# Conv-preact spectral block on one core: images 0 to 3 of the next batch loaded during the attention, and the "+1" of the scaling factors moved from GpSimd to ScalarE

## The reference

```
n    = groupnorm(x)                     # 32 groups of 8 columns, over all images and rows
xn   = instance_norm(n)                 # per image
k, q = spectral_conv(xn) -> 64 x 64     # low modes only, 8 x 8 corners
v    = spectral_conv(xn) -> 256 x 256
att  = softmax(q k^T * 64) v            # over the 64 images of a batch
att  = instance_norm(att) + n
mix  = spectral_conv(instance_norm(att), 32 x 32 corners)
skip = instance_norm(att) * w
out  = instance_norm(instance_norm(mix + skip)) + att
y    = x + out
```

## Time and profile before

| | us |
|---|---|
| median of 3 runs (range) | 658.64 (658.28 to 662.75) |
| profiled execution: its own time | 657.47 |
| its span in the trace | 655.5 |
| busy: PE / DVE / ACT / POOL | 619.2 / 486.5 / 336.7 / 356.0 |
| transfers | 136.32 MB |
| PE's granted clock, mean of the execution | 0.988 of full speed |

### The profile page before, as it was taken

The page is one execution under the profiler, slowest core; times in us unless marked ns, Lnnn a source line. Parts: engine busy times, 40 slices in busy tenths (PEclk is TensorE's granted clock), DMA queues, the critical chain, the costliest instruction groups (busy, mean ns, idle before and its releaser), DMA issues.

```text
span 655.5 us, 14804 instructions
## 1 busy us (share of the span) xinstructions
PE 619.2 (94%) x5584; PEld 556.6 (85%) x5584; DVE 486.5 (74%) x1095; ACT 336.7 (51%) x730; POOL 356.0 (54%) x430
## 2 busy tenths in 40 slices
PE   9999899899999899989999999989999989996994
PEld 8999798699999889879999878978898987985773
DVE  4666876788776777678777767768887778768896
ACT  6888343465665523365666634256576662333331
POOL 0260035969970013897993002498899000369995
PEclk9999999999999999999999999999999999997998
DMA  9991000999999400399999910069999970004686
GB/s 322 335 386 56 1 1 7 313 314 331 302 308 326 161 1 1 102 341 302 315 338 304 319 39 1 2 240 309 334 292 320 314 249 1 1 33 174 252 311 259
DMA packets 72215, 136.32 MB, mean 208 GB/s; under 512 B 5905, under 2 KB 6417, under 8 KB 72145
## 3 DMA queue, kind: packets, MB, share of 16 engines
q1 hardware_dynamic: 72144, 135.38, 60.9%
HBM read 68.25 MB, written 67.11 MB: 206 GB/s over the span
## 4 chain that ended last, share of the span: by engine, by line
PE 55%; DVE 15%; DMA 10%; POOL 10%; ACT 3%; issue 3%; SPq 3%; POOLq 0%; DVEq 0%; ACTq 0%
PE psY L354 21%; PE psP L408 12%; POOL X L801 8%; PE psY L377 7%; DMA X<-in_x 6%; PE psT L393 5%; DMA out<-X 4%; DVE QP L889 4%; DVE Y L853 3%; ACT SQ L566 3%; PE psP L377 2%; SPq L324 2%; DVE SQ L853 1%; PE psP L454 1%; DVE X L853 1%
## 5 line engine op out<-in xcount | busy, mean ns | idle before, releaser
L801 POOL TENSOR_TENSOR X<-X,ALPHA 128x512 f32<-128x512 f32 x244 | 254.4, 1078 | 17.4 <-DVE IM L1086 15.4
L354 PE MATMUL psY<-FWD,X 128*128 128x128 f32 x2048 | 247.8, 279 | 10.3 <-DMA X<-in_x 10.2
L354 PEld LDWEIGHTS psY<-FWD,X 128*128 128x128 f32 x2048 | 234.9, 192 | 26.4 <-issue 18.5
L889 DVE TENSOR_REDUCE QP<-SQ 128x32 f32<-128x512 f32 x256 | 162.2, 679 | 49.6 <-ACT SQ L566 49.4
L853 DVE TENSOR_TENSOR X<-X,psP 128x512 f32<-128x512 f32 x192 | 126.3, 684 | 54.3 <-PE psP L408 24.7
L566 ACT ACTIVATE SQ<-X 128x512 f32<-128x512 f32 x256 | 146.2, 621 | 14.7 <-DMA X<-in_x 7.4
L408 PE MATMUL psP<-INVW,T 64*128 64x256 f32 x768 | 141.1, 402 | 9.5 <-DVE X L853 8.6
L779 POOL TENSOR_TENSOR Y<-Y,OMEGA 128x256 f32<-128x256 f32 x32 | 23.8, 743 | 192.1 <-ACT Y L570 191.9
L588 ACT ACTIVATE T<-psT,BIA,SCL 128x256 f32<-128x256 f32 x128 | 65.3, 560 | 108.9 <-PE psT L393 104.3
L408 PEld LDWEIGHTS psP<-INVW,T 64*128 64x128 f32 x768 | 93.1, 190 | 28.7 <-issue 12.4
L558 ACT ACTIVATE Y<-psY 128x512 f32<-128x512 f32 x128 | 76.2, 596 | 57.1 <-PE psY L354 56.6
(11 more groups left out here) (197 smaller groups left out, 446.4 us busy)
## 6 DMA issues: line engine op xcount, KB each, us to landing
X<-in_x SPq DMA_DIRECT2D x116, 512.0 KB, 5.4
out<-X SPq DMA_DIRECT2D x116, 512.0 KB, 4.8
X<-in_x SPq DMA_DIRECT2D x24, 256.0 KB, 3.9
out<-X SPq DMA_DIRECT2D x24, 256.0 KB, 3.5
INVH<-t_inv_h SPq DMA_DIRECT2D x1, 256.0 KB, 9.0
LW<-in_low_w SPq DMA_DIRECT2D x1, 204.0 KB, 7.5
GWT<-t_w SPq DMA_DIRECT2D x1, 192.0 KB, 9.8
FWD<-t_fwd SPq DMA_DIRECT2D x1, 128.0 KB, 2.2
```

What stands on the lines that cost most here:

```text
L354: last = mm(psY[p % 2][:, (2 * i + c) * 128:(2 * i + c + 1) * 128], X[:, 2 * p + i, a, c * 128:(c + 1) * 128], FWD[:, a, :], start=a == 0, ...
L801: P.tensor_tensor(v, v, al, MUL).then_inc(x_scaled, 1)
L889: V.tensor_reduce(QP[:, 4 * (k % 2) + place(n) % 4, :], SQ[:, n % RING, :].rearrange("p (a g j) -> p g a j", a=HC, j=GW), AX.XY, ADD).then ...
```

## The change

`AHEAD = 4` images of the next batch are loaded a second time. While the attention of batch b runs, SP waits until GpSimd has added groups 0 to 4 of `S`, and loads images 0 to 3 of batch b+1 with one transfer of 1 MB into `Y[:, 1, 0, 8:40, :]`, the place of the weighted modes of groups 1 to 4. The forward transform and the squares of these four images read that copy. Their ordinary load into `X`, after the store of the old images, stays where it was; GpSimd's scaling waits for it now.

For the factors, GpSimd now does only the product `c * r`; a new ScalarE instruction adds the one (`add_one`, semaphore `one_added`). GpSimd makes the product of group g+1 inside group g, ahead of its third image (ahead of the seventh in group 4), and that of group 0 ahead of the last `add_products` of the attention. ScalarE's `add_one` of group g+1 stands in unit 2g, behind `keep_t` (in unit 9 for group 5), in every batch.

```diff
+        AHEADf = Y[:, 1, 0, 8:8 + 8 * AHEAD, :].rearrange("p i u -> p (i u)").rearrange("p (i n) -> p i n", n=HC * W)
+        AHEADx = AHEADf.rearrange("p i (a w) -> p i a w", a=HC)
...
+        def image(nb, n):
+            return AHEADx[:, n, :, :] if nb and n < AHEAD else X[:, n, :, :]
+
+        def flat_image(nb, n):
+            return AHEADf[:, n, :] if nb and n < AHEAD else Xf[:, n, :]
+
+        def image_in(nb, n):
+            return (ahead_in, 16 * nb) if nb and n < AHEAD else (loaded(n), 16 * nb + 16)
...
             def batch(b, more):
+                if more:
+                    sp.wait_ge(products, 8 * b + 1 + AHEAD)
+                    sp.dma_start(AHEADf, x_v[b + 1, :, 0:AHEAD, :]).then_inc(ahead_in, 16)
                 for q in range(PAIRS):
...
-                    pe.wait_ge(loaded(2 * p + i), 16 * nb + 16)
+                    pe.wait_ge(*image_in(nb, 2 * p + i))
...
-                act.wait_ge(loaded(n), 16 * nb + 16)
+                act.wait_ge(*image_in(nb, n))
...
-                nc.scalar.activation(SQ[:, n % RING, :], Xf[:, n, :], ACT.Square).then_inc(squared, 1)
+                nc.scalar.activation(SQ[:, n % RING, :], flat_image(nb, n), ACT.Square).then_inc(squared, 1)
...
+            def add_one(b, g):
+                act.wait_ge(alpha_made, 8 * b + g + 1)
+                al = ALPHA[:, g % 2, :, :].rearrange("p i g -> p (i g)")
+                nc.scalar.activation(al, al, ACT.Identity, bias=ONES[:, 0:1], scale=1.0).then_inc(one_added, 1)
...
                 mode_powers(b, SPLIT)
+                add_one(b, 0)
                 low_piece(b, 0)
...
+                    if u < 2 * NG - 2 and u % 2 == (u // 2 == SPLIT - 1):
+                        add_one(b, u // 2 + 1)
                     if not more and u in (2, second(b) + 5):
                         vector_alphas(b, int(u > 2))
...
             def alphas(b, g):
 
-                al = ALPHA[:, g % 2, :, :]
-                P.tensor_tensor(al, over(MR[:, 5, 0:1], [[0, 8], [1, GROUPS]]),
+                if g in (0, SPLIT):
+                    pool.wait_ge(c2_kept, 2 * b + 1 + (g > 0))
+                P.tensor_tensor(ALPHA[:, g % 2, :, :], over(MR[:, 5, 0:1], [[0, 8], [1, GROUPS]]),
                                 over(C2[:, 8 * g:8 * g + 1], [[1, 8], [0, GROUPS]]), MUL).then_inc(alpha_made, 1)
-                pool.wait_ge(alpha_made, 16 * b + 2 * g + 1)
-                P.tensor_tensor(al, al, over(ONES[:, 0:1], [[0, 8], [0, GROUPS]]), ADD).then_inc(alpha_made, 1)
-                pool.wait_ge(alpha_made, 16 * b + 2 * g + 2)
...
                     weigh(b, g)
+                    if g == SPLIT:
+                        alphas(b, 0)
                     add_products(b, g)
                 behind = {2: SPLIT + 1, 8 if b < B - 1 else 3: SPLIT + 2}
                 for g in range(NG):
-                    if g in (0, SPLIT):
-                        pool.wait_ge(c2_kept, 2 * b + 1 + (g > 0))
-                    if g >= 2:
-                        pool.wait_ge(x_scaled, scaled_by_pool(b, 8 * g - 8))
-                    alphas(b, g)
+                    pool.wait_ge(one_added, 8 * b + g + 1)
                     for i in range(8 * g, 8 * g + 8):
+                        if i == 8 * g + (6 if g == SPLIT - 1 else 2) and g < NG - 1:
+                            if b or g:
+                                pool.wait_ge(x_scaled, scaled_by_pool(b, 8 * g))
+                            alphas(b, g + 1)
                         if i == 4 * LAG + 12 and b < B - 1:
                             pool.wait_ge(coef_made, 2 * b + 2)
```

More of the change, by code:

```diff
@@ L19 @@
 QRING = 8
+AHEAD = 4
 HALVED = (0, PAIRS - 2, PAIRS - 1)
@@ L178, in spectral_block @@
         store_first = {q: sem(f"store_first{q}") for q in HALVED}
+        ahead_in = sem("ahead_in")
         fwd_in = sem("fwd_in")
@@ L235, in spectral_block @@
         alpha_made = sem("alpha_made")
+        one_added = sem("one_added")
         vector_alpha = sem("vector_alpha")
@@ L354, in forward @@
                             last = mm(psY[p % 2][:, (2 * i + c) * 128:(2 * i + c + 1) * 128],
-                                      X[:, 2 * p + i, a, c * 128:(c + 1) * 128], FWD[:, a, :],
+                                      image(nb, 2 * p + i)[:, a, c * 128:(c + 1) * 128], FWD[:, a, :],
                                       start=a == 0, stop=a == HC - 1)
@@ L788, in alphas @@
             def alphas(b, g):
-                al = ALPHA[:, g % 2, :, :]
-                P.tensor_tensor(al, over(MR[:, 5, 0:1], [[0, 8], [1, GROUPS]]),
+                if g in (0, SPLIT):
+                    pool.wait_ge(c2_kept, 2 * b + 1 + (g > 0))
+                P.tensor_tensor(ALPHA[:, g % 2, :, :], over(MR[:, 5, 0:1], [[0, 8], [1, GROUPS]]),
                                 over(C2[:, 8 * g:8 * g + 1], [[1, 8], [0, GROUPS]]), MUL).then_inc(alpha_made, 1)
-                pool.wait_ge(alpha_made, 16 * b + 2 * g + 1)
-                P.tensor_tensor(al, al, over(ONES[:, 0:1], [[0, 8], [0, GROUPS]]), ADD).then_inc(alpha_made, 1)
-                pool.wait_ge(alpha_made, 16 * b + 2 * g + 2)
             def scale_x(b, i):
+                if b and i < AHEAD:
+                    pool.wait_ge(loaded(i), 16 * b + 16)
                 v = X[:, i, :, :].rearrange("p a (g j) -> p a g j", j=GW)
```

## The result

| | before | changed |
|---|---|---|
| median of the runs, us | 659.2 (4 runs) | 676.08 (4 runs, 674.9 to 691.56) |
| ratio to before | | 1.0221, 95% interval 1.0177 to 1.0265 |
| profiled execution, its span, us | 657.47, 655.5 | 675.06, 673.0 |
| PE's mean granted clock | 0.988 | 0.974 |
| transfers, MB | 136.32 | 139.45 |

A ratio here leaves out runs over 1.5% above the fastest of their kernel: of the changed kernel the one of 691.56 us, which the experiments give another reading.

What follows compares the result with a forecast made beforehand. PE's unbroken run was taken to bound batches 0 to 2, GpSimd and DVE the last. Terms 9.5 - 1.1 + 0.3 = +8.7 us on 658.6 gave 667.3 us, 664 to 670 in this case; overall range 660 to 675.

Steps and rivals of the forecast that it cites:

- The stall of unit 6: Batches 0 to 2: ScalarE's add_one waits for GpSimd's late product, so PE starts spread later; 3.3 + 3.3 + 2.9 = +9.5 us.
- the loads' 0.5: Batch 0, unit 4: pair 3's forward transform can move forward by 0.5 us and no more.
- The clock: PE after its idle time in unit 6: no slower work counted in the forecast's sum, left to rival 3.
- rival 3: PE's clock falls after the unit 6 stall, about 2 to 2.5 us per batch: +7, so 674 us; chance 0.17.
- The loads ahead: Hand-overs of three batches: unit 3's waits of 5.7 us go, but later pairs are late; -1.1 us, bounds 0 and -5.7.
- One premise: DMA near the hand-over: the trace shows no mixed stretch of stores and loads above 357 GB/s.
- rival 1: Transfers have room: the three hand-overs give back 5.7 us, unit 6's stall stays; +4 to +6, so 663 us; chance 0.2.
- pair 3 would be late next: Batch 0, unit 4: pair 3's reload, issued at 126.26, lands at 131.7; its forward transform began at 132.2.
- The last batch: Second coefficients +1.0 us, two late waits of DVE on GpSimd -0.7; sum +0.3 us, between -3 and +3.
- The second coefficients: Last batch, DVE: they begin at 598.5 instead of 597.49, behind ScalarE's add_one waiting for GpSimd; +1.0 us.
- the 0.7 us that I took: Last batch: GpSimd no longer holds DVE, so two late waits of 0.35 us and the like go; -0.7 us.

Runs made afterwards that it cites:

- experiment 3: The changed kernel with GpSimd making the product of group 4 at the start of group 3, ahead of its wait for the coefficients: 676.26 us, ratio 1.0162.
- 6: experiment 3 plus GpSimd waiting for DVE's multiplication of the energies in all batches but the last: 658.38 us, ratio 0.9946.
- 7: The changed kernel with ScalarE adding the one behind the squares of odd units, plus GpSimd's wait for DVE's energies: 655.21 us, ratio 0.9943.
- Eleven: The changed kernel plus GpSimd's wait for DVE's multiplication of the energies in all four batches: 678.35 us, ratio 1.0288.
- twelve: Eleven plus six extra multiplications of 256 columns that keep PE busy in unit 6 of the first three batches: 665.83 us, ratio 1.0094.
- experiment 10: The changed kernel without loads ahead, ScalarE's ones at the end of odd units, GpSimd waiting for DVE's energies in all batches: 656.27 us, ratio 0.9955.

## Why the prediction was right and wrong

**The stall of unit 6: right.** The chain came step by step: `add_one` at 148.65, `spread` at 152.26, against 152.6 in the working without the loads' 0.5. PE waits 3.01 us three times, 9.0 in all; the sum had 9.5. Experiments 3, 6 and 7 take the wait away in two ways, and the batches without a held instruction fall back to 158 to 160 us.

**The clock: wrong, the step that failed.** The forecast gave PE's idle of 3 us no consequence and left that to rival 3, with 0.17. It argued from the gap of 2.44 us in unit 3, after which 16 matmuls took 2.02 us. One such gap was too little to argue from. All three stalls were followed by a lower clock. From unit 6 to unit 7 PE's rows slip by 12.2 us in sum, 3.2 more than the idle time, and to unit 8 by another 5.2: 8.4 us, where rival 3 had 7. Eleven against twelve gives 6.9 for the same. What spoke for the rival was the nearer row: a gap followed by work at 0.58. The Trainium skill, "TensorE: Matmul & The Clock Gate", section "What's actually happening", has an idle PE fall to 1.2 GHz. These three places agree with that. Shorter idle times went both ways: nothing followed the 2.44 us of the earlier trace rows, nor 2.53 us in batch 2 of experiment 10 (16 forward matmuls in 2.02 us), but 2.47 us in batch 0 of the same profile cost clock, and in batch 1 after the change even 1.87 us did (16 forward matmuls in 2.44 us, a granted clock of 0.50 from 298 to 300 us). What makes the difference I haven't tested.

**The loads ahead: right in kind.** Forecast -1.1 us; -0.5 alone (interval -4.5 to +2.3), -2.4 with the stalls away, which isn't clear of noise. One premise was misread: stores and loads together do pass 357 GB/s, from 466 to 472 us of the kernel before they moved 374, still under the 387 of loads alone. The sum goes by the times of the issues and not by it; it was an argument against rival 1. That pair 3 would be late next came true to 0.1 us. In the change itself the stretch up to unit 6 even became 1.8 us longer over three batches: 2.4 longer in batch 1, where the clock fell behind the 1.87 us, 0.1 longer in batch 2 and 0.7 shorter in batch 0.

**The last batch: wrong sign, small.** The second coefficients came 0.7 us later (forecast 1.0), and the forecast was +0.3 for the whole; it was -2.7, within the bound of -3 that was named. That GpSimd's lighter work reached DVE further than the 0.7 us that I took is the likely cause, argued and not shown.

Sum by the profile: idle 9.0, clock 8.4, hand-overs 1.8, behind unit 8 0.7, last batch -2.7, start 0.4: 17.6, the span's 17.5. The stall was the right half, the clock is the missing one. That the last batch took back nearly all that the hand-overs and the rest added (-2.7 against +2.9) was luck: the forecast had +0.3 and -1.1 there.

**What no case held: DVE shut out.** By taking one instruction and two waits on itself per group from GpSimd, the change joins GpSimd's runs: behind the DVE instruction of experiment 3 GpSimd went on for 9 us without a gap, now for 18. The profiled run of the change has no long instruction, so its 17.6 us do not need it. The run of 691.56 us would be explained by one, but it was not profiled: argued, not shown. Shown are seven such instructions of 17.9 or 18.5 us in the profiles of five kernels with gapless runs: in 5 of the 12 gapless batches 0 to 2, and in 2 of the 7 gapless last ones. There are none in the three batches each of the eight kernels that wait or pause there, nor in the profiles of the two kernels in which GpSimd adds the one itself. Whether the kernel before is sometimes hit, for at most the 9 us to its next pause, stays open.

## What to carry to other kernels

A wait that moves to another engine costs what is queued behind it there. The place of an instruction in the order decides: the same late product cost some 17 us (stall and clock) ahead of ScalarE's squares and nothing behind them. Price an idle time of TensorE together with the slower work after it; here the second part was nearly as large as the first. And look at who shares something with an engine before its small pauses are removed: they may be the only places where another one is sure to get in.

## What was not expected of the hardware

- A DVE instruction with its tensors in SBUF doesn't always take turns with GpSimd's. It can be held until GpSimd pauses: 17.92 us (five times), 18.53 (twice), and in the last batches of eleven and ten 5.67 and 3.45 us, each ending within 0.3 us of the end of GpSimd's run. In other last batches it gets in behind one instruction of a run that goes on (0.87 to 1.06 us). DVE's instructions with one operand in PSUM ran at 0.68 us beside the same GpSimd work.
- What decides isn't in the rows. In batches 0 to 2 the instruction starts 0.13 to 0.16 us ahead of GpSimd's next scaling where it is held, and 0.14 to 0.17 us where it is free (119.26 and 119.41 held, 119.37 and 119.52 free).
- The granted clock fell after each of three idle times of 3.0 us, and stayed at 1.00 when the same time held six extra multiplications whose results nobody reads.
